# Edge sums of a graph layer: unit tables as plain numbers, and a ring refilled by the engine that owns it

## The reference

```python
gathered = edge_val[:, None] * x[edge_col]
support = jax.ops.segment_sum(gathered, edge_row, num_segments=N)
h = jnp.concatenate([x, support], axis=1)
out = h @ W + b
return jax.nn.relu(out)
```

## Time and profile before

| | |
|---|---|
| median of three runs | 1248.14 us (1246.35 to 1250.51) |
| span of the profiled execution | 1260.4 us |
| the profiled execution's own time | not given |
| TensorE busy | 1002.4 us (80%) |
| VectorE, ScalarE, GpSimd busy | 680.7, 598.6, 630.3 us |

### The profile page before, as it was taken

The page is one execution under the profiler, slowest core; times in us unless marked ns, Lnnn a source line. Parts: engine busy times, 40 slices in busy tenths (PEclk is TensorE's granted clock), DMA queues, the critical chain, the costliest instruction groups (busy, mean ns, idle before and its releaser), DMA issues.

```text
span 1260.4 us, 21882 instructions
## 1 busy us (share of the span) xinstructions
PE 1002.4 (80%) x5493; PEld 810.6 (64%) x5494; DVE 680.7 (54%) x1493; ACT 598.6 (47%) x1559; POOL 630.3 (50%) x601
## 2 busy tenths in 40 slices
PE   3889579975676777776767557469999999999995
PEld 1456345554555566565655435368999999999995
DVE  8999834432555555555555357943444444444441
ACT  0535234459656676676666445323333343333331
POOL 2473376665666666566666662213433433433431
PEclk8889789996787888789788867778999999999998
DMA  7112222322222222223222343972222222222221
GB/s 157 36 30 84 59 88 88 91 90 80 88 80 87 85 85 88 80 89 90 83 87 85 92 155 122 368 228 48 35 41 35 34 42 34 34 42 34 36 41 18
DMA packets 53869, 103.07 MB, mean 82 GB/s; under 512 B 14923, under 2 KB 36240, under 8 KB 51612
## 3 DMA queue, kind: packets, MB, share of 16 engines
q0 software_dynamic: 30448, 67.69, 21.4%
q1 hardware_dynamic: 22408, 30.48, 7.8%
q10 hardware_dynamic: 932, 3.95, 0.9%
HBM read 83.96 MB, written 18.13 MB: 81 GB/s over the span
## 4 chain that ended last, share of the span: by engine, by line
PE 50%; DVE 14%; another core or an unknown queue 11%; issue 9%; ACT 7%; SPq 3%; DMA 2%; POOL 2%; DVEq 1%; ACTq 0%; POOLq 0%
PE ps L848 15%; PE ps L838 15%; PE ps L705 10%; ACT arena_e L939 3%; PE ps L753 3%; PE ps L716 2%; DVE arena_a L1262 2%; DVE arena_a L1256 2%; DVE arena_c L1343 1%; SPq L454 1%; PE ps L828 1%; POOL arena_c L560 1%; PE ps L648 1%; PE ps L625 1%
## 5 line engine op out<-in xcount | busy, mean ns | idle before, releaser
L560 POOL DMA_INDIRECT arena_c<-y_d,arena_e x397 | 394.4, 994 | 221.9 <-SPq L455 113.3
L705 PE MATMUL ps<-arena_c,arena_e 128*125 x892 | 282.1, 453 | 164.5 <-SPq L458 56.4
L705 PEld LDWEIGHTS ps<-arena_c,arena_e 128*125 128x125 f32 x892 | 184.4, 222 | 243.6 <-issue 218.9
L939 ACT ACTIVATE arena_e<-arena_e 128x125 f32<-128x125 bf16 x446 | 202.3, 509 | 119.2 <-remote 64.6
L1343 DVE TENSOR_TENSOR arena_c<-arena_c,ps 125x256 f32 x223 | 92.6, 415 | 269.2 <-remote 150.3
L592 POOL DMA_INDIRECT out<-node,bn x56 | 100.9, 1802 | 250.8 <-DVE node L1626 225.5
L1065 ACT ACTIVATE arena_d<-ps,small 128x128 f32<-128x128 f32 x448 | 121.5, 382 | 181.8 <-PE ps L838 140.6
L848 PE MATMUL ps<-arena_c,arena_d 128*128 x896 | 205.5, 383 | 0.2 <-issue 0.2
L848 PEld LDWEIGHTS ps<-arena_c,arena_d 128*128 128x128 f32 x896 | 167.9, 192 | 21.7 <-issue 0.6
L838 PEld LDWEIGHTS ps<-node,arena_d 128*128 128x128 f32 x896 | 105.8, 194 | 2.6 <-DVE node L1618 1.2
L838 PE MATMUL ps<-node,arena_d 128*128 128x128 f32 x896 | 106.1, 277 | 0.8 <-DVE node L1618 0.8
(11 more groups left out here) (344 smaller groups left out, 1319.8 us busy)
## 6 DMA issues: line engine op xcount, KB each, us to landing
arena_a<-in_W SPq DMA_DIRECT2D x8, 1024.0 KB, 12.2
arena_c<-y_d,arena_e POOLq DMA_INDIRECT x397
arena_c<-in_W SPq DMA_DIRECT2D x5, 1024.0 KB
arena_c<-in_W ACTq DMA_DIRECT2D x3, 1024.0 KB
x<-in_x SPq DMA_DIRECT2D x5, 560.0 KB
z_d<-x SPq DMA_DIRECT2D x5, 560.0 KB
out<-x SPq DMA_DIRECT2D x5, 560.0 KB
y_d<-arena_c SPq DMA_DIRECT2D x15, 125.0 KB
```

Of the source, the lines that this page charges most:

```text
L560: pool.indirect_dma_start(ring[:, b % GR, :], None, io["y_d"], bass.IndirectOffsetOnAxis(gix[:, at:at + 1], 0)).then_inc(gth[b % GR], 16)
L705: mm = nc.tensor.matmul(unit_sums(u), sel[(2 * u + j) % SR], ring[:, ds(at + j, 1), :].rearrange("p a c -> p (a c)"), start=(j == 0), stop ...
L939: nc.scalar.activation(sel[b % SR], hot[b // 8 % 2][:, :, b % 8], ACT.Copy, scale=wcols[:, b:b + 1]).then_inc(selm, 1)
```

## The change

The tables are kept as plain integers, one row of 228 numbers each, on different partitions of one buffer: `u_landed` (the count of landed superblocks that a unit needs), `u_place` (its first ring place), `u_last` (the number of units after which a superblock is done) and `u_tile`. Loads fetch eight neighbours of a row at once (four on VectorE) into registers. Packing on VectorE and taking apart on the engines are gone, and so are the checks that a loaded value is within bounds.

SyncE no longer frees ring places. GpSimd, before it refills a place, loads the counts itself (eight at a time) and waits on g_mm. It counts `freed` up as well, which nothing waits for any more. TensorE's waits before a unit are written in another order, each ahead of one of the two address computations, and three waits of the mix attention that stood in front of each tile's matmuls stand once in front of all segments.

```diff
@@ -442,17 +442,7 @@
             def load_w2(e):
                 sp.dma_start(W2[:, e, :, :], io["W2"][e]).then_inc(w2_in, 16)
 
-            sp.wait_ge(u_rows, 1)
-            left = {}
             for s in range(SB):
-                d = s - (RS - RL)
-                if d >= 0:
-                    if d % 3 == 0:
-                        packed = sp.value_load(nrow[0:1, d // 3:d // 3 + 1], min_val=0, max_val=2 ** 24 - 1)
-                        for i in range(3):
-                            left[d + i] = (packed >> 8 * i) & 255
-                    sp.wait_ge(g_mm, sp.compute_val(left.pop(d) + 1))
-                    sp.sem_inc(freed, 1)
                 for b in range(2 * s, min(2 * s + 2, EB)):
                     sp.wait_ge(gth[b % GR], 16 * (b // GR + 1))
                 sp.sem_inc(landed, 1)
...
@@ -551,9 +541,17 @@
             for k in range(YB):
                 pool.wait_ge(y_out[k], 16 * len(range(k, NT, YB)))
             pool.wait_ge(gix_ready, 1)
+            pool.wait_ge(u_rows, 1)
+            left = {}
             for b in range(EB):
-                if b % 2 == 0:
-                    need(pool, freed, b // 2 - RS + 1)
+                d = b // 2 - RS
+                if b % 2 == 0 and d >= 0:
+                    if d % UL == 0:
+                        _, left[0] = nc.values_load_multi_w_load_instructions(
+                            u_last[0:1, d:d + UL], engines=[mybir.EngineType.Pool], min_val=1, max_val=UP + NT,
+                            skip_runtime_bounds_check_because="a count of units, at least one")
+                    pool.wait_ge(g_mm, pool.compute_val(left[0][d % UL] & 255))
+                    pool.sem_inc(freed, 1)
                 if b == GR - 1:
                     pool.wait_ge(e_tr, 2)
                 at = (2 * (b // 2 // BQ) + b % 2) * BQ + b // 2 % BQ
...
@@ -688,21 +686,26 @@
             mm.then_inc(e_tr, 1)
             pe.wait_ge(e_rec, 3)
 
-            blocks = {}
+            places, landings = {}, {}
 
             def sum_edges(u):
-                if u % 3 == 0:
-                    packed = pe.value_load(srow[0:1, u // 3:u // 3 + 1], min_val=0, max_val=2 ** 24 - 1)
-                    for i in range(3):
-                        blocks[u + i] = pe.compute_val((packed >> 8 * i) & 255)
-                s = blocks.pop(u)
-                at = nc.s_assert_within(pe.compute_val((s & (RS - 1)) * 2), 0, GR - 2,
-                                        skip_runtime_bounds_check_because="three bits, doubled")
-                pe.wait_ge(landed, pe.compute_val(s + 1))
+                if u % UL == 0:
+                    n = min(UL, EU - u)
+                    _, places[0] = nc.values_load_multi_w_load_instructions(
+                        u_place[0:1, u:u + n], engines=[mybir.EngineType.PE], min_val=0, max_val=GR - 2,
+                        skip_runtime_bounds_check_because="three bits, doubled")
+                    _, landings[0] = nc.values_load_multi_w_load_instructions(
+                        u_landed[0:1, u:u + n], engines=[mybir.EngineType.PE], min_val=1, max_val=SB,
+                        skip_runtime_bounds_check_because="one to SB, clipped by the vector engine")
+                at, last = places[0][u % UL], landings[0][u % UL]
+                blocks = [ring[:, ds(at + j, 1), :].rearrange("p a c -> p (a c)") for j in range(2)]
+                pe.wait_ge(landed, pe.compute_val(last & 255))
+                pe.lower_ap(blocks[0])
+                need(pe, g_acc, u - 1)
+                pe.lower_ap(blocks[1])
                 pe.wait_ge(selm, 2 * u + 2)
-                need(pe, g_acc, u - 1)
                 for j in range(2):
-                    mm = nc.tensor.matmul(unit_sums(u), sel[(2 * u + j) % SR], ring[:, ds(at + j, 1), :].rearrange("p a c -> p (a c)"),
+                    mm = nc.tensor.matmul(unit_sums(u), sel[(2 * u + j) % SR], blocks[j],
                                           start=(j == 0), stop=(j == 1))
                 mm.then_inc(g_mm, 1)
 
...
@@ -722,17 +725,17 @@
                 sum_edges(n)
             for u in range(G0, G1):
                 sum_edges(u)
+            pe.wait_ge(bd_ready, 1)
+            pe.wait_ge(qk_act, OC * 7)
+            pe.wait_ge(hc_ready, OC)
 
             def channel_rows(t):
-                pe.wait_ge(hc_ready, OC)
-                pe.wait_ge(qk_act, OC * 7)
                 need(pe, a_h, t)
                 for j in range(OC):
                     mm = nc.tensor.transpose(psf[0:T, 128 * j:128 * j + 128], HC[:, j, T * t:T * t + T], ident)
                 mm.then_inc(p_h, 1)
 
             def channel_sums(t):
-                pe.wait_ge(bd_ready, 1)
                 need(pe, a_s, t)
                 for j in range(OC):
                     mm = nc.tensor.matmul(psf[0:T, 1024 + 128 * j:1152 + 128 * j], HC[:, j, T * t:T * t + T], bd[:, j, :],
...
@@ -1226,22 +1229,15 @@
             def unit_rows():
                 v.wait_ge(u_mm, 1)
                 V.tensor_scalar(ubase, ps[:, 3, 0:UP], float(T), None, ALU.mult)
-                V.tensor_scalar(utile, ps[0:1, 3, 0:UP], NT - 1.0, None, ALU.min)
-                V.tensor_tensor(uneed_f, iota_u[0:1, :], ps[0:1, 4, 0:UP], ALU.add)
+                V.tensor_scalar(u_tile, ps[96:128, 3, 0:UP], NT - 1.0, None, ALU.min)
+                V.scalar_tensor_tensor(u_last, iota_u[64:96, :], 1.0, ps[64:96, 4, 0:UP], ALU.add, ALU.add)
                 chain(V.tensor_tensor(usb, iota_u, ps[:, 3, UP:2 * UP], ALU.subtract))
                 chain(V.tensor_scalar(usb, usb, SB - 1.0, None, ALU.min))
                 V.tensor_scalar(usel[:, 0, :], usb, pcol, None, ALU.is_equal)
                 V.tensor_scalar(usel[:, 1, :], usb, pcol2, None, ALU.is_equal)
-                by3 = [a[0:1, :].rearrange("p (a d) -> p a d", d=3) for a in (usb, uneed_f)]
-                for a, out in zip(by3, (srow, nrow)):
-                    pk = upack[:, 0:UP // 3]
-                    chain(V.scalar_tensor_tensor(pk, a[:, :, 2], 256.0, a[:, :, 1], ALU.mult, ALU.add))
-                    chain(V.scalar_tensor_tensor(out[0:1, :], pk, 256.0, a[:, :, 0], ALU.mult, ALU.add))
-                by4 = utile.rearrange("p (a d) -> p a d", d=4)
-                pk = upack[:, 0:UP // 4]
-                chain(V.scalar_tensor_tensor(pk, by4[:, :, 3], 32.0, by4[:, :, 2], ALU.mult, ALU.add))
-                chain(V.scalar_tensor_tensor(pk, pk, 32.0, by4[:, :, 1], ALU.mult, ALU.add))
-                chain(V.scalar_tensor_tensor(trow[0:1, :], pk, 32.0, by4[:, :, 0], ALU.mult, ALU.add))
+                V.tensor_scalar(u_landed, usb[0:32, :], 1.0, None, ALU.add)
+                chain(V.tensor_copy(u_place, usb[32:64, :]))
+                chain(V.tensor_scalar(u_place, u_place, RS - 1, 1, ALU.bitwise_and, ALU.logical_shift_left))
                 v.sem_inc(u_rows, 1)
 
             v.wait_ge(e_slot, 1)
...
@@ -1327,15 +1323,16 @@
 
                 if u % 4 or u >= EU:
                     return
-                packed = v.value_load(trow[0:1, u // 4:u // 4 + 1], min_val=0, max_val=32 ** 4 - 1)
-                for i in range(min(4, EU - u)):
-                    rows[u + i] = v.compute_val((packed >> 5 * i) & 31)
+                n = min(4, EU - u)
+                _, tiles = nc.values_load_multi_w_load_instructions(u_tile[0:1, u:u + n], engines=[mybir.EngineType.DVE], min_val=0, max_val=NT - 1,
+                                                                    skip_runtime_bounds_check_because="clipped to NT - 1, a count")
+                for i in range(n):
+                    rows[u + i] = tiles[i]
 
             def add_sums(u):
                 if u == 0:
                     digits(0)
-                t = nc.s_assert_within(rows.pop(u), 0, NT - 1,
-                                       skip_runtime_bounds_check_because="each digit is clipped to NT - 1")
+                t = rows.pop(u)
                 part = ACC[:, ds(t, 1), :].rearrange("p a c -> p (a c)")
                 v.lower_ap(part)
                 v.wait_ge(g_mm, u + 1)
```

More of the change, by code:

```diff
@@ L54 @@
 RS = 8
-RL = 3
+UL = 8
 BQ = 100
@@ L229, in build @@
         cut = cutter(ED[:, 3700:])
-        trow, srow, nrow = [cut(n, I32) for n in (UP // 4, UP // 3, UP // 3)]
+        urow = cut(UP, I32)
+        u_landed, u_place, u_last, u_tile = [urow[p:p + 32, :] for p in (0, 32, 64, 96)]
         cut = cutter(A[:, 11500:])
@@ L236, in build @@
         ucol = cut(3)[0:NT, :]
-        utile, uneed_f, upack = [cut(UP)[0:1, :] for _ in range(3)]
         place_hot = A[0:NT, 10000:10000 + NK * 64].bitcast(BF16).rearrange("p (k n) -> p k n", k=NK)
```

## The result

The changed kernel takes **1244.93 us** (median of 20 runs, 1241.98 to 1262.16) against 1250.78 of the kernel before (20 runs, 1246.35 to 1262.44): a ratio of **0.995, interval 0.993 to 0.997**. Run again on another chip it was 0.991 (0.987 to 0.994). So it is faster by half a per cent to one per cent. 1226 us was forecast, 22 us less than before: right in sign, but the change is 6 us by the first comparison and 12.5 by the second.

The account below looks back on a forecast made before the run. No engine was full in the 626 us before 782; late TensorE signals were taken to hold that stage. Terms −1 −2 + 0 + 6 −25 = −22 us from the 1248.1 median gave 1226 us, range 1185 to 1265.

Parts of the forecast that it names:

- late signals: 156 to 782 us: VectorE's 40 remote waits each end one slow SyncE step (0.70 us) sooner, −25 us; ends 0 and 111.
- The view it rested on: Edge-sum stage: late signals, slow SyncE and trains of gathers come together; from 158 to 169 us trains alone made none.
- Tables, −1: Table building: seven chained operations of some 0.25 us go, three wider ones come, two of them chained; −1 us.
- TensorE 0 and VectorE −2: Sequencers at unit matmuls and adds: TensorE's fewer loads hidden, 0; VectorE's shorter register work −2 us, ends 0 and −6.
- GpSimd +6: Ring refill: GpSimd now loads counts and waits itself; its 24 loads cost +6 us, ends 0 and 62.
- The signals stay late: Rival, chance 0.20: gather trains or profile recording hold TensorE's signals, SyncE is another victim; 1245 to 1251 us.
- The signals come on time: Rival, chance 0.13: SyncE's stream is the whole cause, then gathers bound the stage; up to −111 us, 1135 to 1190.
- A load of eight costs eight: Rival, chance 0.12: eight-value loads cost eight single loads on TensorE and GpSimd; +44 us, 1289, or 1264 with signals cut.
- GpSimd becomes the late one: Rival, chance 0.10: GpSimd's in-order wait breaks each gather train, signals as late as before; +19 us, 1264.

## Why the prediction was wrong

The reading that late signals hold the stage up was right; the step that failed is the term "late signals", −25 us: what makes them, and with it the size. That the sign came out right was in part luck: the part of the change that was to bring the gain, SyncE's freeing, is worth nothing that can be seen, and what gain there is went with the parts of TensorE and VectorE, put at 0 and −2.

- *Late signals, −25.* "If each of the 40 waits ends one such step sooner": SyncE's slow steps did vanish with its loop, yet the waits are 142.4 us in 41 instead of 150.3 in 40, 8 us less and not 25; with SyncE freeing again they are 143.5. A hold does not end when SyncE is done; by the runs without gathers and with paced ones, what decides is how fast GpSimd's gathers follow each other. By the runs with idle instructions SyncE's count as a small share of a common load, an estimated 6 to 8 ns each and not 0.70 us per hold. The upper end of the term, 111 us, took the 1.25 us at which GpSimd issues for what a gather needs: at the 1.42 to 1.46 at which signals begin to go through, 397 of them need 564 to 580 us, and by that estimate only 27 to 43 of the 607 could have come back. The last add ends 12.7 us earlier in the profile (767.6 instead of 780.3), not 20 to 30.
- *The view it rested on.* From 158 to 169 us no signal was late, with gathers in a row but without SyncE's loop, and that was taken as a sign that "the trains alone did not make them". In the changed kernel SyncE frees nothing, and the first late signal is due at the same time: the unit summed at 170.16 to 171.19 is added at 174.75, after 4.98 us of waiting (the profile names TensorE there). The run with SyncE's copies has its one late signal there too. With the paced runs beside it, the likelier reading is that a backlog of gathers grows in these 20 us, and that SyncE's loop only began when it was full. That the ring's 16 places are full for the first time then is a third thing that begins together with them, and was not set apart. Two things that begin together in one execution are one observation.
- *Tables, −1.* As forecast. From its first operation the building took 138.92 to 143.93 before; the first and last rows of after, in VectorE's timeline:

```profile
139.83 0.40 DVE L1231 TENSOR_SCALAR arena_a<-ps 128x228 f32<-128x228 f32 x1 [2.71 <-PE ps L668]
...
143.75 3.36 DVE L1279 TENSOR_TENSOR arena_c<-arena_c,small 125x3072 f32<-125x3072 f32 x1 [0.26 <-DVE arena_e L1240]
```

  That is 3.92 us instead of 5.01, 1.1 less. It began 0.9 us later in this execution, so the first gather starts at 149.0 in both.
- *TensorE 0 and VectorE −2.* Undone alone they cost 6 and 8 us with wide intervals, but show no worth where hardly anything is held: as time on the path they were counted about rightly. That they count by adding to the common load fits the runs with idle instructions but is not shown for these two engines. TensorE's loads now take 33 us (28 times 593 and 587 ns) instead of the 17 that the prediction reckoned with; that, too, is hidden.
- *GpSimd +6.* Its loads, 566 ns, and waits fit beside running gathers: with that part undone the time is the same (0.989 beside 0.991 and 0.995). The gaps between gathers grew from 0.31 us (100.4 us in 322) to 0.33 (108.8 in 329).
- *The rivals.* "The signals stay late" was the closest; its sum of 1245 to 1251 holds the 1244.93 but for a hair (by the second comparison the change is larger). Its thought, that SyncE is one more victim, is right of the slow steps; that SyncE's stream had no part is what the run with idle traffic excludes. "The signals come on time" falls with the 142.4 us. "A load of eight costs eight" falls: 593 ns and not 2.4 us. By the Trainium skill's some 200 ns per register (Runtime: NRT & Kernel Launch, "Instruction fetch mechanics") it would be an estimated 1.6 us; the trace does not agree. Its slope on TensorE is (593 − 302) / 7 = 42 ns for each value more, and that is what counts here. "GpSimd becomes the late one" falls with the paced runs: 0.11 us more per gather cost almost nothing.

What gathers and sequencer instructions share is open. The recorder of the instructions is one candidate: it would be a load that counts instructions. The Trainium skill (NOTIFIC — the notification-queue block, "Overflow: three behaviours, one of which stalls the engine") says that inside the block the pipeline holds back rather than lose a record. No run here tells whether it has a part: the profiled execution of after, 1247.21 us, lies among its other runs, but span and clock were recorded in these as well, so none is known to have gone without the recorder.

## What to carry to other kernels

A wait whose releaser is "remote" and whose producer was done long ago is not that producer's fault: look for an engine that issues in long stretches beside it, and pace it before you tune the waiting ones. Here a pause of 0.17 us in front of each gather took the changed kernel from 0.991 or 0.995 to 0.978, more than the whole change gave; on the kernel before, with its 2041 instructions more, it gave nothing. So where signals are held, count the register and semaphore instructions beside the path too: 1791 idle ones on SyncE cost about 1%.

## What had not been expected of the hardware

- GpSimd's gathers of 128 rows delay the semaphore signals of TensorE and the instructions of SyncE when they follow each other in 1.25 or 1.36 us, partly at 1.42, hardly at 1.46 (14.3 us of waits instead of 142.4) and next to not at 1.55 (4.5 us); with a quarter of the bytes as much as with all (169.6 us), and with one wait of 3.7 us when SyncE copies as many bytes.
- The first delay starts after some 20 us of gathers in a row (15 of them, from 149.0 to 169.8, before). The later ones need no such run-up: most in the kernel before come behind 6 to 10 gathers in a row, 7 to 13 us.
- A load of table values into registers takes 302 ns for one (TensorE), 343 for four (VectorE), 566 to 593 for eight (GpSimd, TensorE).
- A slower GpSimd made the kernel faster: 1.42 us instead of 1.25 per gather, 1227.54 us instead of some 1244, on other chips.
